# LayerNorm gains and shifts folded into the weights that follow, and the first feed-forward layer in plain fp32 on 64 rows per image

## The chip, the core and the metric

The kernel runs on one core of a Trainium2 chip. A core has a matrix engine (PE, with its weight loads shown apart as PEld), a vector engine (DVE), a scalar engine (ACT), a general engine (POOL) and a queue engine (SP) that issues DMAs. Each engine runs its own instructions in order; they meet only at semaphores. The metric is the device time of one execution in microseconds, and lower is better.

## The reference, cut to what matters

Four layers follow each other on eight images of 16 by 16 positions with 64 channels. The change lies in the third and in what the fourth reads from it:

```python
# layer 3 (its end), x after the hexagonal attention
x = _layernorm(x + attn_out, g1, beta1)
ff = jax.nn.relu(x @ w1.T + b1) @ w2.T + b2      # 64 -> 256 -> 64
x = _layernorm(x + ff, g2, beta2)
# layer 4, input x, all batch norms folded as scale and shift
h = jax.nn.relu(_bn(conv1x1(x, w1) + b1))        # 64 -> 128
h = jax.nn.relu(_bn(conv3x3(h, w2, groups=32) + b2))
h = conv1x1(h, w3) + b3                          # 128 -> 64
return jax.nn.relu(x + h)
```

`_layernorm` is (x - mean) * rsqrt(var + eps) * gain + shift over the 64 channels. The first two layers are self-attentions over the 256 positions of an image.

## The kernel before

Channels lie on partitions. Two images stand above each other, image 0 of a pair on partitions 0 to 63 and image 1 on 64 to 127, so there are four pairs of 256 columns. From the end of the third layer on, two pairs make one group `gr` of 512 columns, which fills one PSUM bank. Weights of a 64 by 64 layer are laid on the diagonal of a 128 by 128 matrix, so that one matmul serves both images.

Each engine's program is written out by hand, so the order in the code is the order on the engine. Nothing is scheduled or planned by a tool.

**Preparation.** `prepare2` on PE (L925) multiplies weights together while the hexagonal attention is being prepared: `outc` (the output projection with the centring matrix), `w2c` (the second feed-forward layer with it) and the two centred biases of `cb`. ACT copies them from PSUM at L488 to L490, in front of the copy `att_hi` (L492) that the attention waits for. Behind `prepare2`, PE runs matmuls on zeros (`keep_warm`, L834), then `batch_norm_rows` (L1085), one more `keep_warm`, and then `cast` (L1052), which spreads the attention weights over the channels for DVE's `weighted_values` (L738).

**A LayerNorm,** number n = 0 to 3: 0 and 1 are the first one of groups 0 and 1, 2 and 3 the second one. PE has already put the centred input into `D_BANK[gr]`. ACT squares it (`squares`, L501), PE averages the squares over 64 channels (`variance`, L1092), ACT takes the logarithm and the exponential of minus one half of it (`inverse_std`, L507 and L511), DVE multiplies (`layer_norm`, L771, writes `xhat`) and in a second pass applies gain and shift (L774, writes `x1` or `x2`). `x2` has the place of `yT`.

**The first feed-forward layer** works on halves in the type fp32r, whose products keep fewer bits. `halves` on DVE rounds `x1` to its upper half (L783) and stores the rest (L787), for each image in a tile `xs[:, gr, i, :]` of its own: upper half on the image's own 64 partitions, rest on the other 64. The weights are split in the same way into `w1_hi` and `w1_lo`, each holding w1 twice. So for each image and each half of the 256 hidden channels two matmuls over 128 rows give the layer: eight for a group (L1104). `centre_r`, made by four ACT copies at L478, then puts the centred `x1` into `D_BANK` (L1111, two matmuls), and the second layer adds to it (L1116, plain fp32, images 0 and 1 on output partitions 0 to 63 and 64 to 127). The ReLU with bias b1 is ACT's for image 0 (L516) and DVE's for image 1 (L793).

**The fourth layer.** `conv1` (L1128, weights `c1s` = w1 times the batch norm's scale), ReLU on ACT into `strips` with 32 partitions at a time (`conv1_out`, L529), two shifted copies for each strip on DVE (`shifts`, L307), the 3 by 3 convolution as four column tiles of 32 outputs (`conv2`, L1140, and `conv2_last`, L1150), ReLU on ACT (L541, L536), `conv3` (L1163), and `finish` on DVE, which adds bias and `x2` (L807) and takes the ReLU (L810). There are three results: columns 0 to 511, and twice 256 columns, each with its own store. The programs of PE, ACT and DVE from the first LayerNorm on end in lists of calls (L1184 to L1207, L545 to L562, L812 to L825).

Of the kernel before, what the change touches and what calls it, by code (L numbers as in the profile page):

```python
# [14 lines left out]
F32 = mybir.dt.float32  # L15
# [51 lines left out]
def build(nc, t, out):  # L67

    ctx = ExitStack()
    with ctx:  # L70
# [47 lines left out]
        centre_r = ctx.enter_context(nc.sbuf_tensor("centre_r", [128, 2, 128], F32R))  # L118
# [38 lines left out]
        w1_hi = ctx.enter_context(nc.sbuf_tensor("w1_hi", [128, DFF], F32R))  # L157
        w1_lo = ctx.enter_context(nc.sbuf_tensor("w1_lo", [128, DFF], F32R))


        xs = ctx.enter_context(nc.sbuf_tensor("xs", [128, GROUPS, 2, 512], F32R))
# [3 lines left out]
        xhat = sb("xhat", 128, 2, 512)  # L165
        x1 = sb("x1", 128, GROUPS, 512)
        x2 = yT[:, :, :].rearrange("p (g j) n -> p g (j n)", g=GROUPS)
# [13 lines left out]
        x3 = sq[:, :, :].rearrange("p a n -> p (a n)")  # L181
# [41 lines left out]
        xhat_sb, ln_out = sem("xhat_sb"), sem("ln_out")  # L223
        stacked = sem("stacked")
        w1_split, x_upper, x_lower = sem("w1_split"), sem("x_upper"), sem("x_lower")
# [72 lines left out]

        AFFINE = [("L2_conv_g1", "L2_conv_beta1"), ("L2_conv_g2", "L2_conv_beta2")]
# [82 lines left out]
        def _(act):  # L382
# [130 lines left out]
            def relu_ff(gr):  # L513
                for h in range(FH):
                    act.wait_ge(ff_ps, 2 * FH * gr + h + 1)
                    s.activation(ffh[:, gr, h, 0, :], bank[h], ACT.Relu,  # L516
                                 bias=col("L2_conv_b1", h)).then_inc(ff_act, 1)

            def conv1_out(c):

                act.wait_ge(c1_ps, c + 1)
                if c == 0:
                    act.wait_ge(bn_ready, 3)
                    act.wait_ge(zeroed, 3)
                if c >= 2:
                    act.wait_ge(c2_ps, c - 1)
                for r in range(CONV_BLOCKS):
                    h = slice(32 * r, 32 * r + 32)
                    s.activation(strips[32:64, c % 2, r, :, 1:1 + SIDE, :],  # L529
                                 bank[c][h, :].rearrange("p (j a b) -> p j a b", j=2, b=SIDE),  # L530
                                 ACT.Relu, bias=bnsh[h, 0:1]).then_inc(c1_sb, 1)
# [15 lines left out]
            squares(1)  # L547
            inverse_std(1)
            relu_ff(0)
# [15 lines left out]
        def _(dve):  # L565
# [105 lines left out]
            for n in range(SLOTS):  # L671
# [89 lines left out]
            for i in range(2):  # L761
                v.tensor_tensor(c1s[:, i, :], c1[:, i, :], bank[7][:, 0:128], ALU.mult)
# [4 lines left out]
            def layer_norm(n):  # L767
                gr = n % 2
                dst, (gain, shift) = (x1, x2)[n // 2], AFFINE[n // 2]
# [7 lines left out]
            def halves(gr):  # L777


                dve.wait_ge(ln_out, gr + 1)  # L780
                for i in range(2):
                    own = slice(64 * i, 64 * i + 64)
                    v.tensor_copy(xs[own, gr, i, :], x1[own, gr, :]).then_inc(x_upper, 1)  # L783
                for i in range(2):
                    own, other = slice(64 * i, 64 * i + 64), slice(64 - 64 * i, 128 - 64 * i)
                    dve.wait_ge(x_upper, 2 * gr + i + 1)
                    v.tensor_tensor(xs[other, gr, i, :], x1[own, gr, :], xs[own, gr, i, :].bitcast(F32),  # L787
                                    ALU.subtract).then_inc(x_lower, 1)

            def relu_ff(gr):  # L790
                for h in range(FH):
                    dve.wait_ge(ff_ps, 2 * FH * gr + FH + h + 1)
                    v.tensor_scalar(ffh[:, gr, h, 1, :], bank[FH + h], col("L2_conv_b1", h), 0.0,  # L793
                                    ALU.add, ALU.max).then_inc(ff_dve, 1)
# [21 lines left out]
            halves(1)  # L816
# [11 lines left out]
        def _(pe):  # L828
# [96 lines left out]
            def prepare2():  # L925
# [8 lines left out]
                for k, name in enumerate(("L2_conv_out_b", "L2_conv_b2")):  # L934
                    ins = mm(b[:, 256 + k:257 + k], centre, col(name), start=True, stop=True)
# [142 lines left out]
            def batch_norm_rows():  # L1078
# [3 lines left out]
                for k in range(2):  # L1082
                    b = bninv[:, k:k + 1]
                    column = bass.AP(tensor=b.tensor, offset=b.offset, ap=[list(b.ap[0]), [0, 128]])
                    ins = mm(bank[7][:, 128 * k:128 * k + 128], column, ident, start=True, stop=True)  # L1085
                ins.then_inc(bnrow_ps, 1)
# [7 lines left out]
            def feed_forward1(gr):  # L1094

                pe.wait_ge(w1_split, 2)
                pe.wait_ge(stacked, 1)
                for i in range(2):
                    pe.wait_ge(x_lower, 2 * gr + i + 1)
                    for h in range(FH):  # L1100
                        if gr:
                            pe.wait_ge(ff_act if i == 0 else ff_dve, h + 1)
                        for w in (w1_hi, w1_lo):
                            ins = mm(bank[FH * i + h], w[:, 128 * h:128 * h + 128], xs[:, gr, i, :],  # L1104
                                     start=w is w1_hi, stop=w is w1_lo)
                        ins.then_inc(ff_ps, 1)

            def feed_forward2(gr):

                for i in range(2):  # L1110
                    mm(D_BANK[gr], centre_r[:, i, :], xs[:, gr, i, :], start=i == 0, stop=False)  # L1111
# [9 lines left out]
            def conv1(c):  # L1121
                gr, i = c // 2, c % 2
                pe.wait_ge(ln_out, 3 + gr)
# [4 lines left out]
                mm(bank[c], c1s[:, i, :], x2[:, gr, :], start=True, stop=True).then_inc(c1_ps, 1)  # L1128
# [25 lines left out]
            def conv3(n, i):  # L1154

                b, columns = RESULTS[n]
                gr = n > 0
                if i == 0:
                    pe.wait_ge(c2_sb, 2 * gr + 1)
                else:  # L1160
                    pe.wait_ge(c2_sb, n + gr + 2)
                c2 = c2out.rearrange("p g i n -> p i g n")[:, i, gr, columns.start - 512 * gr:columns.stop - 512 * gr]
                ins = mm(b[64 * i:64 * i + 64, :], table["c3"], c2, start=True, stop=True)  # L1163
# [22 lines left out]
            out_sums(3)  # L1186
            variance(1)
            feed_forward1(0)
            feed_forward2(0)
            variance(2)  # L1190
            feed_forward1(1)
# [98 lines left out]
```

## Time and profile before

| | us |
|---|---|
| median of 3 runs | 128.46 |
| lowest and highest | 128.42, 128.50 |
| span of the profiled execution | 125.2 |

The profile is of one execution, and its span runs from the first to the last instruction. The time of that execution itself isn't listed; what lies around the span is taken as the median minus the span, 3.26 us. The granted clock of PE is 1.000 over the whole span.

| engine | busy us | share of the span | instructions |
|---|---|---|---|
| PE | 105.7 | 84% | 600 |
| DVE | 93.7 | 75% | 246 |
| ACT | 68.5 | 55% | 164 |
| POOL | 42.7 | 34% | 43 |

The chain that ended last (followed back from the last instruction, at each step to what released it) is PE for 42% of the span, DVE for 29% and ACT for 15%. PE's busy time counts overlapping records, so what a change is worth is read from the chain and the timeline of the stage, not from these shares. A plain fp32 matmul shows as two MATMUL records, one in fp32r as one. A time in the timeline is the start from the span's beginning, and the duration reaches to the end of the last record of a row.

### The profile page before, as it was taken

The page shows a single profiled execution, that of the slowest core. Times are in us where ns is not written, and L with a number is a line of the kernel's source. Part 1 is how long each engine was busy: PE and PEld are TensorE (multiplying, and loading weights), DVE is VectorE, ACT ScalarE, POOL GpSimd, SP SyncE. Part 2 cuts the span into 40 slices and gives each one's busy share as a digit, 9 for nine tenths or more (in the row PEclk, how much of TensorE's full clock was granted, in tenths as well). Part 3 has the DMA queues.
Part 4 walks back from the last instruction along what each step waited for, and adds up shares of the span by engine and source line. Part 5 has one row for each costly group of instructions (what it writes and reads, how often), then busy time and mean ns, then how long its engine had stood idle before and what let it go on. Part 6 is the DMA issues. An engine that isn't in the chain of part 4 may idle for free.

```text
span 125.2 us, 1845 instructions
## 1 busy us (share of the span) xinstructions
PE 105.7 (84%) x600; PEld 64.4 (51%) x600; DVE 93.7 (75%) x246; ACT 68.5 (55%) x164; POOL 42.7 (34%) x43
## 2 busy tenths in 40 slices
PE   4988999899999988599399957998697992998990
PEld 1475957577777775365035634985353530221350
DVE  1078999878888669737979989793878739998733
ACT  3137985687979775637503310025534579986530
POOL 8996004351608217095500079991000000000000
PEclk9999999999999999999999999999999999999999
DMA  3960000000000000000000000000000000000022
GB/s 105 309 280 0 0 0 0 5 5 0 0 0 0 0 5 0 0 0 0 5 0 0 0 3 0 0 0 0 0 0 0 0 5 3 0 0 0 5 84 84
DMA packets 1593, 2.81 MB, mean 22 GB/s; under 512 B 176, under 2 KB 1200, under 8 KB 1584
## 3 DMA queue, kind: packets, MB, share of 16 engines
q1 hardware_dynamic: 1152, 2.02, 4.5%
q10 hardware_dynamic: 432, 0.67, 1.6%
q8 instruction: 5, 0.08, 0.3%
q14 instruction: 4, 0.03, 0.1%
HBM read 2.17 MB, written 0.52 MB: 22 GB/s over the span
## 4 chain that ended last, share of the span: by engine, by line
PE 42%; DVE 29%; ACT 15%; issue 8%; DMA 2%; POOL 1%; ACTq 0%; DVEq 0%
PE bank L913 5%; DVE strips L307 5%; PE bank L883 4%; DVE probn L604 4%; ACT prob L411 4%; PE bank L1074 3%; PE bank L1104 3%; DVE ffh L253 3%; PE bank L1116 3%; PE bank L1052 3%; ACT strips L529 3%; DVE nmax L595 3%; DMA p<-in_p 2%; PE duo L1140 2%; DVE qkprod L738 2%
## 5 line engine op out<-in xcount | busy, mean ns | idle before, releaser
L411 ACT ACTIVATE prob<-bank,nmax 128x256 f32<-128x256 f32 x32 | 14.8, 469 | 8.2 <-DVE nmax L595 7.8
L883 PE MATMUL bank<-kz,q 128*128 128x256 f32 x64 | 16.4, 383 | 0.3 <-ACT kz L400 0.3
L595 DVE TENSOR_REDUCE nmax<-bank 128x2 f32<-128x512 f32 x16 | 11.0, 689 | 5.7 <-PE bank L883 5.7
L307 DVE COPY strips<-strips 32x480 f32<-32x480 f32 x32 | 12.8, 400 | 3.0 <-ACT strips L529 2.4
L883 PEld LDWEIGHTS bank<-kz,q 128*128 128x128 f32 x64 | 11.5, 190 | 2.1 <-issue 0.5
L604 DVE TENSOR_SCALAR probn<-prob,rrec 128x256 f32<-128x256 f32 x32 | 12.1, 421 | 0.6
L529 ACT ACTIVATE strips<-bank,bnsh 32x512 f32<-32x512 f32 x16 | 10.9, 680 | 2.1 <-PE duo L1140 1.1
L893 PE MATMUL bank<-pv,probn 128*128 128x128 f32 x64 | 10.0, 278 | 2.1 <-DVE probn L604 2.1
L501 ACT ACTIVATE sq<-bank,cb 128x512 f32<-128x512 f32 x4 | 2.7, 687 | 15.3 <-PE bank L1074 11.0
L1140 PE MATMUL duo<-strips,ctaps 128*32 128x512 f32 x72 | 8.3, 596 | 3.2 <-DVE strips L307 3.2
L893 PEld LDWEIGHTS bank<-pv,probn 128*128 128x128 f32 x64 | 7.4, 142 | 4.6 <-DVE probn L604 4.2
L418 ACT ACTIVATE probT<-bank 128x512 f32<-128x512 f32 x16 | 9.4, 596 | 0.1
L346 POOL TENSOR_TENSOR grs<-gvar,minus_half 128x1 f32<-128x1 f32 x4 | 2.7, 683 | 19.2 <-DVE gvar L626 19.2
L913 PE MATMUL bank<-probT,v 128*64 128x256 f32 x64 | 8.5, 390 | 1.0 <-ACT probT L418 1.0
L253 POOL TENSOR_TENSOR qkprod<-q,k 128x768 f32<-128x768 f32 (+1 forms) x4 | 5.8, 1469 | 9.0 <-ACT k L443 9.0
L1052 PE MATMUL bank<-att_hi,head_cast_r 128*128 128x448 f32 x16 | 6.7, 420 | 2.4 <-POOL att_lo L260 1.5
L1140 PEld LDWEIGHTS duo<-strips,ctaps 128*32 128x32 f32 x72 | 2.0, 109 | 9.3 <-DVE strips L307 5.8
L834 PE MATMUL bank<-zeros 128*128 128x512 f32 x8 | 5.1, 741 | 1.6 <-DVE zeros L575 1.6
L411 ACT ACTIVATION_READ_ACCUMULATOR prob<-bank,nmax 128x1 f32 x32 | 6.3, 197 | 0.0
L738 DVE TENSOR_TENSOR ffh<-bank,v 128x128 f32<-128x128 f32 (+1 forms) x24 | 5.5, 304 | 0.6 <-PE bank L1052 0.6
L913 PEld LDWEIGHTS bank<-probT,v 128*64 128x64 f32 x64 | 4.0, 136 | 3.7 <-ACT probT L418 2.1
L1052 PE MATMUL bank<-att_lo,head_cast_r 128*128 128x448 f32 x16 | 5.8, 365 | 0.0
(148 smaller groups left out, 229.3 us busy)
## 6 DMA issues: line engine op xcount, KB each, us to landing
p<-in_p SPq DMA_DIRECT2D x1, 952.0 KB, 7.1
xT<-in_xT SPq DMA_DIRECT2D x4, 128.0 KB, 4.0
p<-in_p ACTq DMA_DIRECT2D x1, 448.0 KB, 5.7
out_dram<-xT SPq DMA_DIRECT2D x1, 256.0 KB, 2.0
out_dram<-xT SPq DMA_DIRECT2D x2, 128.0 KB, 1.7
pv<-in_pv ACTq DMA_DIRECT2D x1, 128.0 KB, 3.2
p<-in_p ACTq DMA_DIRECT2D x1, 79.5 KB, 3.0
```

Of the source, the lines that this page charges most:

```text
L253: return engine.tensor_tensor(products[j][:, k0:k0 + n, :].rearrange("p k (a b) -> p k a b", b=SIDE), rep(q2[:, j, :].rearrange("p (a b) - ...
L307: return engine.tensor_copy(strips[32 * s:32 * s + 32, c % 2, r, :, 1:1 + SIDE, d], strips[32:64, c % 2, r, :, 1:1 + SIDE, f])
L411: s.activation(prob[:, n % 3, b, :], S_BANK[n % 3][:, b * TOK:(b + 1) * TOK], ACT.Exp, bias=nmax[:, n, b:b + 1], accum_out=rsum[:, n, b:b ...
L418: s.activation(flat(probT[:, n % 4, :, :]), T_BANK[n % 2], ACT.Copy).then_inc(probT_sb, 1)
L529: s.activation(strips[32:64, c % 2, r, :, 1:1 + SIDE, :], bank[c][h, :].rearrange("p (j a b) -> p j a b", j=2, b=SIDE), ACT.Relu, bias=bns ...
L595: v.tensor_reduce(nmax[:, n, :], S_BANK[n % 3].rearrange("p (b m) -> p b m", b=BLK), AX.X, ALU.max, negate=True).then_inc(max_ready, 1)
L604: v.tensor_scalar(probn[:, n % 2, b, :], prob[:, n % 3, b, :], rrec[:, n, b:b + 1], None, ALU.mult).then_inc(norm_done, 1)
L883: ins = mm(S_BANK[n % 3][:, b * TOK:(b + 1) * TOK], q[:, b * 128:b * 128 + 128], k, start=True, stop=True)
L893: ins = nc.tensor.transpose(T_BANK[n % 2][:, mb * TOK + b * 128:mb * TOK + b * 128 + 128], probn[:, n % 2, b, mb * 128:mb * 128 + 128], ident)
L913: ins = mm(OUT_BANK[p][64 * i:64 * i + 64, 0:TOK], val[:, 2 * j + mb, 64 * i:64 * i + 64], probT[:, (2 * p + i) % 4, mb, :], start=mb == 0 ...
L1052: ins = mm(CAST_BANKS[m % 2][h][:, 0:NB * 64], w, flat(a[:, c, :, :]), start=a is att_hi, stop=a is att_lo)
L1140: ins = mm(bank[7 - c % 2][32 * r:32 * r + 32, :], ctaps[:, r, ty, :], strips[:, c % 2, r, :, ty:ty + SIDE, :], start=ty == 0, stop=ty == 2)
```

## The change

The gain and the shift of both LayerNorms leave the data and go into weights and biases:

- `w1g` = w1 times gain 1, and `b1f` = b1 plus w1 times shift 1. `centre_g` = the centring matrix times gain 1, and shift 1 is added to the centred bias in `cb`. `c1s` also gets gain 2, and `bnsh1` is the batch norm's shift with shift 2 worked in. `gain2` is a diagonal matrix with gain 2, and `b3f` is the last bias plus shift 2.
- The second DVE pass of each LayerNorm (L774) is gone, and `xhat` keeps all four results.
- `halves`, `w1_hi`, `w1_lo`, `xs` and `centre_r` are gone. The first feed-forward layer is four plain fp32 matmuls for a group, each over the 64 rows of one image, with images 0 and 1 on different rows and in different banks. One fp32 matmul with `centre_g` replaces the two at L1111.
- `conv3` starts each result with a matmul of `gain2` and `xhat`, so `finish` is one DVE instruction instead of two.
- `prepare2` gets three more small matmuls, `batch_norm_rows` one, and ACT two copies into `b1f`.
- On PE, `feed_forward1(0)` goes ahead of `variance(1)` and `feed_forward1(1)` ahead of `variance(2)`. On ACT, `relu_ff(0)` goes ahead of `inverse_std(1)`.

The diff, cut to its core:

```diff
@@ ACT
-            act.wait_ge(tables_in["p1"], 16)
-            for i in range(2):
-                for half in range(2):
-                    h = slice(64 * half, 64 * half + 64)
-                    ins = s.activation(centre_r[h, i, :], centre[64 * i:64 * i + 64, :], ACT.Copy)
-            ins.then_inc(stacked, 1)
...
                     s.activation(cb[:, 0:2], PREP_BANK[:, 256:258], ACT.Copy).then_inc(prep2_sb, 1)
+                    for h in range(FH):
+                        s.activation(b1f[:, h:h + 1], PREP_BANK[:, 258 + h:259 + h], ACT.Identity,
+                                     bias=col("L2_conv_b1", h)).then_inc(affine_b, 1)
...
             squares(1)
+            relu_ff(0)
             inverse_std(1)
-            relu_ff(0)
             squares(2)
@@ DVE
-                    v.tensor_copy(w1_hi[:, :], table["w1T"]).then_inc(w1_split, 1)
-                    dve.wait_ge(w1_split, 1)
-                    v.tensor_tensor(w1_lo[:, :], table["w1T"], w1_hi[:, :].bitcast(F32), ALU.subtract)\
-                        .then_inc(w1_split, 1)
+                    v.tensor_scalar(w1g[:, :], table["w1T"], col("L2_conv_g1"), None, ALU.mult)
+                    v.tensor_scalar(centre_g[:, :], centre, col("L2_conv_g1"), None, ALU.mult)
+                    v.tensor_scalar(gain2[:, :], ident, col("L2_conv_g2"), None, ALU.mult)
+                    v.tensor_tensor(b3f[:, :], col("L3_conv_b3"), col("L2_conv_beta2"), ALU.add)\
+                        .then_inc(affine_w, 1)
...
-                v.scalar_tensor_tensor(out=xhat[:, gr, :], in0=D_BANK[gr], scalar=cb[:, n // 2:n // 2 + 1],
+                v.scalar_tensor_tensor(out=xhat[:, n, :], in0=D_BANK[gr], scalar=cb[:, n // 2:n // 2 + 1],
                                        in1=rstd[:, gr, :], op0=ALU.add, op1=ALU.mult).then_inc(xhat_sb, 1)
-                dve.wait_ge(xhat_sb, n + 1)
-                v.tensor_scalar(dst[:, gr, :], xhat[:, gr, :], col(gain), col(shift), ALU.mult, ALU.add)\
-                    .then_inc(ln_out, 1)
...
-                done(v.scalar_tensor_tensor(out=x3[:, columns], in0=b, scalar=col("L3_conv_b3"),
-                                            in1=x2.rearrange("p g n -> p (g n)")[:, columns],
-                                            op0=ALU.add, op1=ALU.add))
-                v.tensor_scalar(fin[:, columns], x3[:, columns], 0.0, None, ALU.max).then_inc(fin_sb, 1)
+                v.tensor_scalar(fin[:, columns], b, b3f[:, :], 0.0, ALU.add, ALU.max).then_inc(fin_sb, 1)
 
             layer_norm(0)
-            halves(0)
             relu_ff(0)
@@ PE
-                for k, name in enumerate(("L2_conv_out_b", "L2_conv_b2")):
-                    ins = mm(b[:, 256 + k:257 + k], centre, col(name), start=True, stop=True)
+                mm(b[:, 256:257], centre, col("L2_conv_out_b"), start=True, stop=True)
+                mm(b[:, 257:258], centre, col("L2_conv_b2"), start=True, stop=False)
+                mm(b[:, 257:258], centre, col("L2_conv_beta1"), start=False, stop=True)
+                for h in range(FH):
+                    ins = mm(b[:, 258 + h:259 + h], table["w1T"][0:64, 128 * h:128 * h + 128],
+                             col("L2_conv_beta1")[0:64], start=True, stop=True)
...
+                mm(bank[7][:, 256:257], c1[0:64, 0, :], col("L2_conv_beta2")[0:64], start=True, stop=True)\
+                    .then_inc(bnrow_ps, 1)
...
-                for i in range(2):
-                    pe.wait_ge(x_lower, 2 * gr + i + 1)
-                    for h in range(FH):
-                        if gr:
-                            pe.wait_ge(ff_act if i == 0 else ff_dve, h + 1)
-                        for w in (w1_hi, w1_lo):
-                            ins = mm(bank[FH * i + h], w[:, 128 * h:128 * h + 128], xs[:, gr, i, :],
-                                     start=w is w1_hi, stop=w is w1_lo)
-                        ins.then_inc(ff_ps, 1)
+                for h in range(FH):
+                    if gr:
+                        pe.wait_ge(ff_act, h + 1)
+                        pe.wait_ge(ff_dve, h + 1)
+                    for i in range(2):
+                        own = slice(64 * i, 64 * i + 64)
+                        ins = mm(bank[FH * i + h], w1g[own, 128 * h:128 * h + 128], xhat[own, gr, :],
+                                 start=True, stop=True)
+                    ins.then_inc(ff_ps, 1)
...
-                for i in range(2):
-                    mm(D_BANK[gr], centre_r[:, i, :], xs[:, gr, i, :], start=i == 0, stop=False)
+                mm(D_BANK[gr], centre_g[:, :], xhat[:, gr, :], start=True, stop=False)
...
+                own = slice(columns.start - 512 * gr, columns.stop - 512 * gr)
                 if i == 0:
+                    mm(b, gain2[:, :], xhat[:, 2 + gr, own], start=True, stop=False)
                     pe.wait_ge(c2_sb, 2 * gr + 1)
```

The order on PE, from the last matmuls of the attention into the feed-forward stage of group 0, before:

```order
L1074 MATMUL bank<-prob,outc 128x256 x2
L1092 MATMUL duo<-sq,p 128x512 [waits lnv_sb,sq_sb]
L1104 MATMUL bank<-xs,w_hi 128x512 [waits x_lower,stacked,w1_split]
L1104 MATMUL bank<-xs,w_lo 128x512
L1104 MATMUL bank<-xs,w_hi 128x512
L1104 MATMUL bank<-xs,w_lo 128x512
L1104 MATMUL bank<-xs,w_hi 128x512 [waits x_lower]
L1104 MATMUL bank<-xs,w_lo 128x512
L1104 MATMUL bank<-xs,w_hi 128x512
L1104 MATMUL bank<-xs,w_lo 128x512
L1111 MATMUL bank<-xs,centre_r 128x512 x2
L1116 MATMUL bank<-ffh,w2c 64x512 [waits ff_dve,ff_act]
```

The same place after, through to the variance of LayerNorm 2 (`duo<-sq,p` is a variance, `w1g` the first layer, `w2c` the second):

```order
L1053 MATMUL bank<-prob,outc 128x256 x2
L1084 MATMUL bank<-xhat,w1g 128x512 [waits xhat_sb,affine_w]
L1084 MATMUL bank<-xhat,w1g 128x512 x3
L1072 MATMUL duo<-sq,p 128x512 [waits lnv_sb,sq_sb]
L1090 MATMUL bank<-xhat,centre_g 128x512
L1095 MATMUL bank<-ffh,w2c 64x512 [waits ff_dve,ff_act]
L1095 MATMUL bank<-ffh,w2c 64x512
L1095 MATMUL bank<-ffh,w2c 64x512 [waits ff_dve,ff_act]
L1095 MATMUL bank<-ffh,w2c 64x512
L1084 MATMUL bank<-xhat,w1g 128x512 [waits ff_act,ff_dve,xhat_sb,affine_w]
L1084 MATMUL bank<-xhat,w1g 128x512
L1084 MATMUL bank<-xhat,w1g 128x512 [waits ff_dve,ff_act]
```

The variance of LayerNorm 1 has moved from ahead of the first layer to behind it, and the variance of LayerNorm 2 stands two rows behind the last one printed here, behind the first layer of group 1.

The order on ACT from the squares of LayerNorm 2 on is the same in both; after, it reads:

```order
L490 ACTIVATE sq<-bank,cb 128x512 [waits var_ps,d_ps]
L496 ACTIVATE lnv<-duo,epsln 128x512 [waits var_ps]
L500 ACTIVATE rstd<-lnv 128x512 [waits xhat_sb,lnv_sb]
L507 ACTIVATE ffh<-bank,b1f 128x512 [waits ff_ps] x2
L490 ACTIVATE sq<-bank,cb 128x512 [waits var_ps,d_ps]
```

The two ReLUs of group 1 (the row with `ffh`) stand behind the logarithm and the exponential of LayerNorm 2, which wait for that variance.

The end of PE's program after (`gain` is `gain2`; before, the three rows with it are not there, and the rest is the same):

```order
L1119 MATMUL duo<-strips,ctaps 32x512 x11
L1139 MATMUL bank<-xhat,gain 128x512
L1144 MATMUL bank<-ffh,p 64x512 [waits c2_sb] x2
L1129 MATMUL bank<-strips,ctaps 32x256 [waits shifted]
L1129 MATMUL bank<-strips,ctaps 32x256 x23
L1139 MATMUL bank<-xhat,gain 128x256
L1144 MATMUL bank<-ffh,p 64x256 [waits c2_sb] x2
L1139 MATMUL bank<-xhat,gain 128x256
L1144 MATMUL bank<-ffh,p 64x256 [waits c2_sb] x2
```

Each matmul with the gain stands directly ahead of the `conv3` of its result, behind all convolutions that precede it.

## Rows read from the trace of the kernel before

**Rows 1.** Chain that ended last, in order of time: start us, length us, what.
```profile
86.82 0.76 DVE xhat L771
...
87.61 0.56 DVE x L774
...
88.19 0.42 DVE xs L783
...
89.10 0.70 DVE xs L787
...
89.93 2.09 PE bank L1104 x8
...
94.46 0.70 ACT sq L501
...
95.20 1.12 PE duo L1092 x2
96.33 1.88 PE bank L1104 x8
...
98.68 1.94 PE bank L1116 x8
```

**Rows 2.** Timeline of PE: start, us, engine, line, operation [idle before <-releaser].
```profile
84.38 1.02 PE L1092 MATMUL duo<-sq,p 128*128 128x512 f32 x2
...
105.82 2.78 PE L1140 MATMUL duo<-strips,ctaps 128*32 128x512 f32 x24 [2.43 <-DVE strips L307]
108.53 1.98 PE L1128 MATMUL bank<-yT,c1s 128*128 128x512 f32 x4
```

**Rows 3.** Records of one line each, L1140 and L1092: duration ns min/median/max.
```profile
L1140 PE MATMUL duo<-strips,ctaps x72: 592/592/617, 105.8 to 116.2; 128*32 128x512 f32 x72
...
L1092 PE MATMUL duo<-sq,p x8: 592/592/697, 84.4 to 101.9; 128*128 128x512 f32 x8
```

**Rows 4.** Timeline of ACT, group 1 of the feed-forward layer.
```profile
96.36 0.69 ACT L507 ACTIVATE lnv<-duo,epsln 128x512 f32<-128x512 f32 x1 [1.22 <-PE duo L1092]
...
97.62 1.25 ACT L516 ACTIVATE ffh<-bank,p 128x512 f32<-128x512 f32 x2
```

**Rows 5.** Timeline of all engines, the preparation and the start of the attention.
```profile
66.81 0.56 PE L935 MATMUL bank<-p 128*128 128x1 f32 x4
...
67.22 1.96 PE L834 MATMUL bank<-zeros 128*128 128x512 f32 x4
...
68.71 0.58 ACT L492 ACTIVATE att_hi<-att 128x448 fp32r<-128x448 f32 x1 [0.80 <-DVE att L725]
...
69.35 0.68 PE L1085 MATMUL duo<-pv,bninv 128*128 128x128 f32 x4 [0.17 <-DVE sexp L716]
```

**Rows 6.** Timeline of DVE alone, the weighted values of the attention.
```profile
71.94 2.73 DVE L738 TENSOR_TENSOR qkprod<-bank,v 128x192 f32<-128x192 f32 x12
75.07 2.73 DVE L738 TENSOR_TENSOR qkprod<-bank,v 128x192 f32<-128x192 f32 x12 [0.41 <-PE bank L1052]
```

**Rows 7.** Timeline of all engines, the convolutions of the fourth layer.
```profile
107.28 6.72 DVE L307 COPY strips<-strips 32x480 f32<-32x480 f32 x16
...
109.70 2.80 ACT L529 ACTIVATE strips<-bank,bnsh 32x512 f32<-32x512 f32 x4 [0.29 <-PE bank L1128]
...
114.05 2.78 PE L1140 MATMUL duo<-strips,ctaps 128*32 128x512 f32 x24 [0.59 <-DVE strips L307]
```

**Rows 8.** Timeline of all engines, the end.
```profile
116.77 1.45 PE L1163 MATMUL bank<-ffh,p 128*64 128x512 f32 x4
...
118.15 2.80 PE L1150 MATMUL bank<-strips,ctaps 128*32 128x256 f32 x48
...
120.88 1.31 PE L1163 MATMUL bank<-ffh,p 128*64 128x256 f32 x8
...
122.31 0.48 DVE L807 SCALAR_TENSOR_TENSOR sq<-bank,p,yT 128x256 f32<-128x256 f32 x1
122.82 0.29 DVE L810 TENSOR_SCALAR xT<-sq 128x256 f32<-128x256 f32 x1
```

More of the change, by code:

```diff
@@ L116, in build @@
         c1s = sb("c1s", 128, 2, CM)
-        centre_r = ctx.enter_context(nc.sbuf_tensor("centre_r", [128, 2, 128], F32R))
+        centre_g = sb("centre_g", 128, 128)
+        gain2 = sb("gain2", 128, 128)
+        b1f = sb("b1f", 128, FH)
+        b3f = sb("b3f", 128, 1)
+        bnsh1 = sb("bnsh1", 128, 1)
         ctaps = sb("ctaps", 128, CONV_BLOCKS, 3, 32)
@@ L164, in build @@
         rstd = sb("rstd", 128, 2, 512)
-        xhat = sb("xhat", 128, 2, 512)
-        x1 = sb("x1", 128, GROUPS, 512)
-        x2 = yT[:, :, :].rearrange("p (g j) n -> p g (j n)", g=GROUPS)
+        xhat = sb("xhat", 128, 2 * GROUPS, 512)
         ffh = sb("ffh", 128, 2, FH, 2, 512)
@@ L530, in conv1_out @@
                                  bank[c][h, :].rearrange("p (j a b) -> p j a b", j=2, b=SIDE),
-                                 ACT.Relu, bias=bnsh[h, 0:1]).then_inc(c1_sb, 1)
+                                 ACT.Relu, bias=bnsh1[h, :]).then_inc(c1_sb, 1)
             def conv2_out_last():
@@ L761, in _ @@
             for i in range(2):
-                v.tensor_tensor(c1s[:, i, :], c1[:, i, :], bank[7][:, 0:128], ALU.mult)
+                v.scalar_tensor_tensor(out=c1s[:, i, :], in0=c1[:, i, :], scalar=col("L2_conv_g2"),
+                                       in1=bank[7][:, 0:128], op0=ALU.mult, op1=ALU.mult)
+            v.scalar_tensor_tensor(out=bnsh1[:, :], in0=bank[7][:, 256:257], scalar=bninv[:, 0:1],
+                                   in1=bnsh[:, 0:1], op0=ALU.mult, op1=ALU.add)
             v.tensor_tensor(ctaps[:, :, :, :], ctap,
@@ L768, in layer_norm @@
                 gr = n % 2
-                dst, (gain, shift) = (x1, x2)[n // 2], AFFINE[n // 2]
                 dve.wait_ge(rstd_sb, n + 1)
-                v.scalar_tensor_tensor(out=xhat[:, gr, :], in0=D_BANK[gr], scalar=cb[:, n // 2:n // 2 + 1],
+                v.scalar_tensor_tensor(out=xhat[:, n, :], in0=D_BANK[gr], scalar=cb[:, n // 2:n // 2 + 1],
                                        in1=rstd[:, gr, :], op0=ALU.add, op1=ALU.mult).then_inc(xhat_sb, 1)
-                dve.wait_ge(xhat_sb, n + 1)
-                v.tensor_scalar(dst[:, gr, :], xhat[:, gr, :], col(gain), col(shift), ALU.mult, ALU.add)\
-                    .then_inc(ln_out, 1)
-            def halves(gr):
-                dve.wait_ge(ln_out, gr + 1)
-                for i in range(2):
-                    own = slice(64 * i, 64 * i + 64)
-                    v.tensor_copy(xs[own, gr, i, :], x1[own, gr, :]).then_inc(x_upper, 1)
-                for i in range(2):
[L785 to L788, printed above, removed]
             def relu_ff(gr):
+                if gr == 0:
+                    dve.wait_ge(affine_b, FH)
                 for h in range(FH):
-                    dve.wait_ge(ff_ps, 2 * FH * gr + FH + h + 1)
-                    v.tensor_scalar(ffh[:, gr, h, 1, :], bank[FH + h], col("L2_conv_b1", h), 0.0,
+                    dve.wait_ge(ff_ps, FH * gr + h + 1)
+                    v.tensor_scalar(ffh[:, gr, h, 1, :], bank[FH + h], b1f[:, h:h + 1], 0.0,
                                     ALU.add, ALU.max).then_inc(ff_dve, 1)
@@ L1084, in batch_norm_rows @@
                     column = bass.AP(tensor=b.tensor, offset=b.offset, ap=[list(b.ap[0]), [0, 128]])
-                    ins = mm(bank[7][:, 128 * k:128 * k + 128], column, ident, start=True, stop=True)
-                ins.then_inc(bnrow_ps, 1)
+                    mm(bank[7][:, 128 * k:128 * k + 128], column, ident, start=True, stop=True)
+                mm(bank[7][:, 256:257], c1[0:64, 0, :], col("L2_conv_beta2")[0:64], start=True, stop=True)\
+                    .then_inc(bnrow_ps, 1)
             def variance(n):
@@ L1094, in feed_forward1 @@
             def feed_forward1(gr):
[L1096 to L1106 removed]
+                pe.wait_ge(affine_w, 1)
+                pe.wait_ge(xhat_sb, gr + 1)
+                for h in range(FH):
[7 more added lines that the diff above has]
+                    ins.then_inc(ff_ps, 1)
             def feed_forward2(gr):
[L1110 to L1111 removed]
+                mm(D_BANK[gr], centre_g[:, :], xhat[:, gr, :], start=True, stop=False)
                 for h in range(FH):
@@ L1127, in conv1 @@
                     pe.wait_ge(ff_dve, 4)
-                mm(bank[c], c1s[:, i, :], x2[:, gr, :], start=True, stop=True).then_inc(c1_ps, 1)
+                mm(bank[c], c1s[:, i, :], xhat[:, 2 + gr, :], start=True, stop=True).then_inc(c1_ps, 1)
             def conv2(c):
@@ L1161, in conv3 @@
                     pe.wait_ge(c2_sb, n + gr + 2)
-                c2 = c2out.rearrange("p g i n -> p i g n")[:, i, gr, columns.start - 512 * gr:columns.stop - 512 * gr]
-                ins = mm(b[64 * i:64 * i + 64, :], table["c3"], c2, start=True, stop=True)
+                c2 = c2out.rearrange("p g i n -> p i g n")[:, i, gr, own]
+                ins = mm(b[64 * i:64 * i + 64, :], table["c3"], c2, start=False, stop=True)
                 if i:
```

26 lines of the change are left out of this document (11 added, 15 removed).

## The prediction, made before the changed kernel ran

> **What bounds the kernel now.** I read the page's chain first, then the chain in order of time through the last third, then the timelines around each edit. The engines take turns, so an edit pays only where it is the link that ends last. In the first feed-forward stage that link is visible work of the kind that the change removes: `xhat` of group 0 is done at 87.58, DVE then scales it, rounds it twice and subtracts twice, and the first matmul of L1104 starts at 89.93 [rows 1]. From there PE, one ACT square and PE again hold the chain to 100.62 [rows 1]. In the fourth layer DVE's copies and ACT's strips run side by side: the copies of strip set 1 end at half of the row of 6.72 us that began at 107.28, at 110.64, while ACT's first strip of set 2 is ready at about 109.70 + 0.70 = 110.40 [rows 7]. So either engine alone can give back only 0.24 there. At the end PE holds the chain from 114.05 to `conv3` of the last results, and DVE ends it at 123.11 [rows 7, 8].
>
> **Prices on PE.** A plain fp32 matmul of 512 columns is two passes. Two records in 1.02 us with 0.59 for a record [rows 2, 3] put the second start 0.43 after the first, so a matmul holds PE for 0.86, and its result is out 0.16 after that. A first pass after a pause, or after a change of the form of the tile, takes 0.10 more (0.697 against 0.592, [rows 3]). A change of form adds a gap as well: 24 records of 32 output columns start at 105.82 and hold six slots of 0.43, to 108.40, and the next form starts at 108.53 [rows 2]. Together a change costs about 0.2. Column tiles of one form overlap fully: those 24 records, four tiles wide, take 2.78 = 6 x 0.43 + the rest [rows 2], and the eight of L1116 take 1.94 [rows 1].
>
> **The first feed-forward layer.** Before, it is eight passes of about 0.23 for a group, 1.88 in all [rows 1]. After, it is four fp32 matmuls over 64 rows, eight passes of 0.43. No row of this trace has a matmul over 64 rows. If the two images, on different rows and in different banks, overlap as the column tiles do, that is four slots, 1.72. If not, it is 3.44. A gain beyond that would need a pass over 64 rows to be shorter than one over 128. I take the overlap, because the nearest rows, L1116 and L1140, overlap two and four deep. The page TensorE: Matmul & The Clock Gate of the Trainium skill (Part 3) says that row tiles overlap too, with 3.07 times measured for four. No row here shows it. At that efficiency of 0.77 a group would cost 0.5 more, an estimate, and the sum would be 130.8.
>
> **Group 0 and group 1 in a row.** DVE's 0.56, 0.42 and 0.43, 0.70 and the rest go: the first matmul moves from 89.93 to about 87.66 [rows 1], 2.27 earlier. What comes behind it on PE is new:
> - first layer, 0.10 + 1.72, to 89.48
> - variance 1, which stood ahead of it: 0.2 + 0.86, to 90.54 (its ACT and DVE steps are off the chain: about 2.4 us to `xhat` 1 at 92.9, needed at 93.4)
> - `centre_g` in fp32: 0.86 instead of two fp32r passes, to 91.40
> - second layer: 0.2 + 1.72, to 93.32, out at 93.48, so ACT's square starts 0.96 earlier than 94.46 [rows 1]
> - first layer of group 1: 0.2 + 1.72, to 95.24
> - variance 2, which now waits for it: 0.2 + 0.86 + 0.16, out at 96.46, against 95.20 + 1.12 = 96.32 before [rows 1].
>
> So by variance 2 the 2.27 are gone and it is 0.14 later. ACT has the logarithm, the exponential and only then the two ReLUs that the second layer waits for, starting 1.26 after the logarithm [rows 4]. The first ReLU ends at about 98.43, PE starts the second layer at 98.5 instead of 98.68 and ends it at 100.4 instead of 100.62. **Net gain 0.2.** What is late next is ACT.
>
> **Fourth layer.** The second DVE pass at 106.70 goes, 0.55, but ACT's first strip ends the wait after 0.24. I take a further gain of 0.2, so the last full convolution starts about 0.4 earlier than 114.05 [rows 7].
>
> **The gain matmuls at the end.** Before, the last convolution pair starts 118.15 - 114.05 = 4.10 after that point [rows 7, 8]. After, PE has six slots (2.58), a change (0.2), `gain2` (0.86), a change (0.2), `conv3` with both images overlapping (0.86; before, image 1 waited for ACT) and 0.1: 4.80. **Loss 0.7.** Nothing hides it: the matmul stands behind the convolution though its inputs are ready long before. Passes of 256 columns hold 0.22 (24 slots' worth of two: 48 records, four wide, in 2.80 [rows 8]). From 120.88, the start of the last `conv3` group, to the end at 122.82 + 0.29 = 123.11 it was 2.23 [rows 8]. After: a gain matmul (0.48), change and `conv3` (0.1 + 0.48), gain matmul (0.58), `conv3` (0.58), 0.2 until DVE starts, and one DVE instruction from PSUM. For that I take 0.48, the row of the PSUM read; the other bound is 0.29, the row from SBUF [rows 8]. That makes 2.9. **Loss 0.67,** or 0.48 at the lower bound. `finish` loses an instruction for each result, but PE, not DVE, is then last.
>
> **The preparation.** DVE's four instructions for weights replace two, at a place where it waits for PE; ACT's four `centre_r` copies go where it is idle. Both are nothing. `prepare2` gets six passes more. Four records hold 67.22 - 66.81 = 0.41 [rows 5], so 0.6, and two changes of form 0.3: the zero matmuls then end at 69.9 and not ahead of the wait that ends at 69.35 [rows 5]. `batch_norm_rows` adds a 64-row matmul, 0.2 and two changes 0.3. The first `cast` comes 1.0 later. It had about 0.2 of slack before DVE's weighted values at 71.94, and DVE waits 0.41 more before 75.07 [rows 6], which absorbs half of what is left. **Loss 0.4,** with bounds 0 and 1.0. ACT's two copies of one column in front of `att_hi` at 68.71 [rows 5] eat its 0.80 of idle time and about 0.2 more, on the same stretch, so they don't add.
>
> **The sum.** Against the profiled execution: -0.2 - 0.2 + 0.7 + 0.67 + 0.4 = +1.4, a span of 126.6. With the 3.26 around it, which no edit touches, that is 129.8, set against the median of 128.46. With changes of form for nothing it would be about 129.0, with twice their price 131.0. The page TensorEngine Tiling of the Trainium skill (Key Properties) says that a change of tiling mode drains the engine. The gap in the rows agrees for column forms; for row forms nothing shows it.
>
> **Rivals.**
> - *Images don't overlap.* Each group's first layer takes 3.44, and both are on the chain: +3.4, 133.2. For it: no row shows 64-row tiles. Against: both column forms overlap. Chance 0.12.
> - *Faster: passes over 64 rows are cheap.* The one mechanism that can turn the sign is the pass price of L1104's successor. If a 64-row pass held 0.21 instead of 0.43, both groups would be 0.86 shorter, and variance 2 would come 1.7 earlier. Then 129.8 - 1.7 = 128.1. It decides from a pass of 0.25 down. Against: matmuls with 32 and with 128 weight columns have the same record, 0.592 [rows 3], so the 512 streamed columns set it and not the share of the array in use. Chance 0.08.
> - *No change: the preparation hides and changes cost nothing.* -0.4 and -0.8: 128.6. Chance 0.08.
> - *The change doesn't do what it says.* DVE does lose its instructions, so only the compiler could merge the images on the same rows. That is the first rival.
>
> **How the numbers follow.** The forecast, 129.8, has 0.72, with its own range of 128.9 to 131.0. The range from 128.1 to 131.0 takes in the faster and the unchanged case, and leaves out the 0.12 without overlap and some of the forecast's edges. About 0.2% (0.26 us) is what a measurement can tell from no change. Faster by more than that: 0.10. Within it: 0.10. Slower: 0.80.
>
> **What would show it.** Right: the first-layer matmuls start near 87.7 plus the delay of the preparation, in pairs; variance 2 comes out behind group 1's first layer, no earlier than before; about 0.7 more between the last full convolution and the last pair; DVE's last instruction waits for PE. Wrong: single 64-row matmuls one after the other (133), or pairs in slots shorter than 0.43 (128), or the first `cast` no later than before.

## The result, and the profile after

The changed kernel is slower: a median of 130.26 us over 13 executions (128.53 to 131.90), against 128.59 us (128.31 to 130.78) for 13 of the kernel before. Taken over the executions of each kernel that are at most 1.5% above its fastest, the ratio is 1.0108 with a 95% interval of 1.0065 to 1.0151.

In most executions of either kernel PE's clock is granted at its lower level (1.2 instead of 2.4 GHz) for one or more stretches, each costing 0.7 to 1.8 us, so spans are compared below for executions with PE at full clock, beside the medians. At full clock the kernel before has a span of 125.2 (the profile shown ahead of the prediction, and two executions measured later, of 126.96 and 127.01 us), the changed one 126.7. The change costs 1.5 us.

The changed kernel's profile has a granted clock of 0.996 and a time of 128.53 us, so 1.8 us lie around its span. The changed kernel's busy times:

```profile
PE 109.7 (87%) x614; PEld 64.5 (51%) x614; DVE 87.0 (69%) x234; ACT 67.6 (53%) x162; POOL 42.8 (34%) x43
```

DVE is 6.7 us less busy and PE 4.0 more. In the chain that ended last, PE went from 42% to 54% of the span. The chain in order of time through the feed-forward stage, which answers [rows 1] (start, length, what):

```profile
87.25 0.76 DVE xhat L765
...
88.15 1.99 PE bank L1084 x8
90.14 1.06 PE duo L1072 x2
91.20 0.86 PE bank L1090 x2
92.05 1.87 PE bank L1095 x8
93.92 1.92 PE bank L1084 x8
95.84 1.07 PE duo L1072 x2
...
96.93 0.70 ACT lnv L496
...
98.91 1.94 PE bank L1095 x8
100.85 1.07 PE bank L1107 x2
```

L1084 is the first layer, L1072 a variance, L1090 the centring and L1095 the second layer. `xhat` of group 0 ends at 88.0, 0.43 later than before, and the first layer starts 0.14 behind it, where it took 2.35 before. From there PE works without a gap to 96.9. Then it waits for ACT, whose logarithm and exponential stand ahead of the ReLUs, and `conv1` follows at 100.85, where it followed at 100.62 before. `xhat` was 0.43 later and `conv1` is 0.23 later, so of the 2.2 us that the first layer gained only 0.2 are left.

The records of the first layer, over 64 rows:

```profile
L1084 PE MATMUL bank<-xhat,w1g x16: 589/589/693, 88.2 to 95.2; 64*128 64x512 f32 x16
```

A pass over 64 rows is as long as one over 128 (0.592 in [rows 3]), and eight of them take 1.99 where eight of them one after the other, 0.43 apart, would take 3.6. So the images overlap in pairs.

The end, which answers [rows 7] and [rows 8] (timeline, the rows of PE, and the last one of DVE):

```profile
114.11 2.78 PE L1119 MATMUL duo<-strips,ctaps 128*32 128x512 f32 x24 [0.65 <-DVE strips L301]
116.82 1.13 PE L1139 MATMUL bank<-xhat,gain 128*128 128x512 f32 x2
117.88 1.08 PE L1144 MATMUL bank<-ffh,p 128*64 128x512 f32 x4
118.89 2.80 PE L1129 MATMUL bank<-strips,ctaps 128*32 128x256 f32 x48
121.61 0.70 PE L1139 MATMUL bank<-xhat,gain 128*128 128x256 f32 x2
122.24 0.65 PE L1144 MATMUL bank<-ffh,p 128*64 128x256 f32 x4
122.83 0.70 PE L1139 MATMUL bank<-xhat,gain 128*128 128x256 f32 x2
123.45 0.65 PE L1144 MATMUL bank<-ffh,p 128*64 128x256 f32 x4
...
124.16 0.48 DVE L787 TENSOR_SCALAR xT<-bank,b3f 128x256 f32<-128x256 f32 x1 [0.73 <-PE bank L1144]
```

From the last full convolution to the pair behind it, L1129, it is 4.78 instead of 4.10. From the start of L1129 to the end it is 5.75 instead of 4.96. Those two are all of the 1.5, since the last full convolution itself starts only 0.06 later than before: the 0.43 lost by `xhat` has been regained on the way, 0.2 in the feed-forward stage and 0.2 in the fourth layer.

### The profile page after: what moved, and what is told of

Same layout as the page of the kernel before. It is cut to its first block, busy times and chain, and to the rows that moved or that the text cites. A ratio compares the mean times of both kernels' runs of the same rounds, so it can differ in the third digit from the quotient of the medians.

```text
span 126.7 us, 1861 instructions
## 1 busy us (share of the span) xinstructions
PE 109.7 (87%) x614; PEld 64.5 (51%) x614; DVE 87.0 (69%) x234; ACT 67.6 (53%) x162; POOL 42.8 (34%) x43
## 4 chain that ended last, share of the span: by engine, by line
PE 54%; DVE 24%; ACT 12%; issue 7%; ACTq 0%; DVEq 0%
DVE strips L301 5%; PE bank L888 5%; PE duo L1119 4%; PE bank L858 4%; DVE qkprod L730 4%; PE bank L809 4%; DVE probn L595 4%; ACT prob L405 3%; PE bank L1053 3%; DVE ffh L249 3%; PE bank L1084 3%; PE bank L1095 3%; PE bank L1031 3%; DVE nmax L586 3%; PE duo L1072 2%
## 5 line engine op out<-in xcount | busy, mean ns | idle before, releaser
L765 DVE SCALAR_TENSOR_TENSOR xhat<-bank,cb,rstd 128x512 f32<-128x512 f32 x4 | 3.0, 750 | 5.6 <-ACT rstd L500 5.4
```

## The experiments

A span "at full clock" is that of the executions whose mean granted clock is at least 0.995. Medians depend on how many executions had stretches at the lower clock, so they say less than these spans; they are given too.

### The end alone: finish_on_dve

```diff
@@ PE, conv3
-                    mm(b, gain2[:, :], xhat[:, 2 + gr, own], start=True, stop=False)
@@ DVE, finish
-                v.tensor_scalar(fin[:, columns], b, b3f[:, :], 0.0, ALU.add, ALU.max).then_inc(fin_sb, 1)
+                done(v.scalar_tensor_tensor(out=x3[:, columns], in0=xhat[:, 2 + gr, own], scalar=col("L2_conv_g2"),
+                                            in1=b, op0=ALU.mult, op1=ALU.add))
+                v.tensor_scalar(fin[:, columns], x3[:, columns], b3f[:, :], 0.0, ALU.add, ALU.max).then_inc(fin_sb, 1)
```

> The changed kernel without its three gain matmuls; gain 2 is applied by DVE in the last step instead (two DVE instructions per result, as in the kernel before). If the gain matmuls are 0.7 us ahead of the last convolution pair and cost the same again behind it, the span falls from 126.7 by 0.7 + 0.78 = 1.5 to about 125.2, and the last instruction of DVE waits for DVE again. Rival: DVE's second instruction per result was what the end waited for, and only the 0.7 comes back (126.0).

Span at full clock 125.3 (one execution of 12, 127.07 us), 1.4 less than the changed kernel. The median is 130.31 (ratio to the kernel before 0.998, interval 0.9934 to 1.0027), because 7 of the 12 had a mean clock of 0.971 to 0.973 and spans of 128.4 to 128.7. The profile is of an execution with a stretch at the lower clock ahead of this place, so its times are later, but the distances hold. Timeline:

```profile
115.77 2.78 PE L1124 MATMUL duo<-strips,ctaps 128*32 128x512 f32 x24 [0.65 <-DVE strips L302]
...
119.81 2.80 PE L1134 MATMUL bank<-strips,ctaps 128*32 128x256 f32 x48
...
124.54 0.35 DVE L792 TENSOR_SCALAR xT<-sq,b3f 128x256 f32<-128x256 f32 x1
```

From the full convolution to the pair it is 4.04 (4.78 in the changed kernel), and from there to the end 5.08 (5.75). Both terms of the gain matmuls come back, 0.74 and 0.67, with DVE carrying two instructions per result again. The rival, that only 0.7 returns, falls.

### ACT's order alone: relu_first

```diff
@@ ACT
             squares(2)
+            relu_ff(1)
             inverse_std(2)
-            relu_ff(1)
```

> The changed kernel with one line moved on ACT: the two ReLUs of group 1 stand ahead of the logarithm and exponential of LayerNorm 2. In the changed kernel's trace the first layer of group 1 is out at 94.98 and 95.84 and ACT is idle from 94.66 to 96.93, while PE waits 1.16 us, to 98.91, for the ReLU. If ACT's order eats the earlier start, the second layer starts at about 97.7 and the span falls by 1.2 to 125.5. Rival: PE's order (the variance behind the first layer) is the bound; then LayerNorm 2 still ends at 99.06 and the gain is below 0.3.

Span at full clock 125.5, 125.5 and 125.7 in three executions of 12, so 1.0 to 1.2 less; median 128.97 (ratio to the kernel before 0.9964, interval 0.9911 to 1.0016). One line takes back what the earlier start had lost. Its place is read best in the profile of both_undone_filled below, which has the same edit and full clock. Timeline of ACT, then of PE:

```profile
94.99 0.69 ACT L508 ACTIVATE ffh<-bank,b1f 128x512 f32<-128x512 f32 x1 [0.37 <-PE bank L1090]
95.85 0.69 ACT L508 ACTIVATE ffh<-bank,b1f 128x512 f32<-128x512 f32 x1 [0.17 <-PE bank L1090]
96.89 0.69 ACT L497 ACTIVATE lnv<-duo,epsln 128x512 f32<-128x512 f32 x1 [0.36 <-PE duo L1078]
```

```profile
95.73 1.12 PE L1078 MATMUL duo<-sq,p 128*128 128x512 f32 x2
96.69 1.02 PE L1096 MATMUL bank<-xhat,centre_g 128*128 128x512 f32 x2
97.64 1.94 PE L1101 MATMUL bank<-ffh,w2c 128*64 128x512 f32 x8
```

Both ReLUs fit into ACT's idle time before the logarithm, which starts when it did in the changed kernel, and the second layer starts at 97.64 instead of 98.91. The rival falls: PE's own order, with the variance behind the first layer, was not what ended last.

### The overlap of the 64-row matmuls: rows128

The weights of each image are padded with zeros to 128 rows, so each matmul takes the rows of both images and multiplies those of the other one by zero.

```diff
+                        v.tensor_scalar(w1g[own, i, :], table["w1T"][own, :], col("L2_conv_g1")[own], None, ALU.mult)
...
-                        ins = mm(bank[FH * i + h], w1g[own, 128 * h:128 * h + 128], xhat[own, gr, :],
+                        ins = mm(bank[FH * i + h], w1g[:, i, 128 * h:128 * h + 128], xhat[:, gr, :],
```

> The changed kernel with the first feed-forward layer over all 128 rows: the weights of each image are padded with zeros on the other image's rows, so no two of its matmuls can overlap; everything else stays. If the 64-row pairs overlap fully, each group needs 3.44 us instead of 1.72, less about 0.4 for the changes of form that fall away: the span grows by 3.0 to 3.4, to about 129.9. Rival: the 64-row matmuls overlap only in their records and the difference is below 1.5.

Span at full clock 129.7 in one execution of 6, 3.0 more (131.47 us; median 134.11, ratio to the kernel before 1.0314, interval 1.0235 to 1.0393). The profile is of another execution, whose granted clock is 1.00 from 86 to 106 us. The chain's two pieces:

```profile
89.78 3.67 PE bank L1087 x8
...
97.03 3.63 PE bank L1087 x8
```

They are 1.68 and 1.71 longer than in the changed kernel. The variances behind them are 0.2 shorter each, as no change of form lies between. The rival of less than 1.5 falls. So rows of one image each, in separate banks, overlap fully in plain fp32.

### The preparation alone: prepare_only

This is the kernel before, with the small matmuls and ACT's two copies added and their results unused.

```diff
+                mm(b[:, 260:261], centre, col("L2_conv_beta1"), start=True, stop=True)
+                for h in range(FH):
+                    ins = mm(b[:, 258 + h:259 + h], table["w1T"][0:64, 128 * h:128 * h + 128],
+                             col("L2_conv_beta1")[0:64], start=True, stop=True)
...
+                mm(bank[7][:, 256:257], c1[0:64, 0, :], col("L2_conv_beta2")[0:64], start=True, stop=True)\
...
+                    for h in range(FH):
+                        s.activation(b1f[:, h:h + 1], PREP_BANK[:, 258 + h:259 + h], ACT.Identity,
+                                     bias=col("L2_conv_b1", h))
```

> The kernel before with only the preparation of the change added (three small matmuls in prepare2, one in batch_norm_rows, two one-column copies on ACT; their results are not used). If the preparation alone costs what the changed kernel's trace shows at the first variance of LayerNorm, the span grows by 0.3 to 0.45 from that of the kernel before. Rival: it is covered by DVE's 0.41 us of waiting and costs under 0.1.

Span at full clock 125.6 in one execution, 0.4 more. In the nine with a clock of 0.985 to 0.987 it is 127.0 to 127.4, median 127.1, against 125.9 to 126.8, median 126.7, in 15 of the kernel before. The rival, less than 0.1, falls. The median of all is no help here (128.89 against 128.90, ratio 1.0012, interval 0.9977 to 1.0048), since the number of stretches at the lower clock moves it more than 0.4.

### Both mended, and the waits of PE filled: both_undone, both_undone_filled, before_filled, after_filled

both_undone is the changed kernel with the edits of finish_on_dve and relu_first. The three others are both_undone, the kernel before and the changed kernel, each with matmuls on zeros put where PE waits:

```diff
+            keep_warm(bank[5], 2)
             head_sums(1)
...
             conv1(1)
+            keep_warm(bank[7], 2)
             conv2(0)
```

> The changed kernel with both mends together: gain 2 applied by DVE in the last step, and group 1's ReLUs ahead of LayerNorm 2's logarithm on ACT. Alone they took the span at full clock from 126.7 to 125.3 and 125.5. If they are separate terms of one chain they add: 124.1 at full clock, 1.1 below the 125.2 of the kernel before. Rival: the 1.2 of the ReLUs is given back by ACT or DVE in the convolutions once the end is short, and the span stays above 124.8.

> As both_undone, with matmuls on zeros put into PE's two long waits: two ahead of the second head_sums (PE idles 2.06 us there in the kernel before) and two ahead of the first 3 by 3 convolution (2.43 us). They take 1.8 us each time and delay nothing. In the profiles in which a stretch was granted half the clock, it began at 62.7 to 63.6 or at 106.4 to 111.4, right behind one of these waits. If the waits cause it, most executions keep the full clock, the span stays at 124.1 and the median falls to about 126. Rival: the chip grants the half clock for another reason (the load), the executions spread as before, and the median is 127.5 or more.

> The kernel before with the same four matmuls on zeros in the same two waits. If the waits cause the half clock, the median falls from 128.5 or 128.9 to 127.0 to 127.3 (the full-clock span of 125.2 plus the 1.8 around it); if not, it stays within 0.3 of 128.6.

> The changed kernel with the same four matmuls on zeros. If the waits cause the half clock, the median falls from 130.3 to about 128.6 (span 126.7), and the difference to before_filled is the change's cost at equal clock, 1.5. If not, it stays near 130.2.

| kernel | span at full clock | median us | executions at full clock |
|---|---|---|---|
| both_undone | 124.1 | 127.57 | 2 of 6 |
| both_undone_filled | 124.1 | 125.88 | 6 of 6 |
| before_filled | 125.2 | 127.01 | 10 of 12 |
| after_filled | 126.7 | 128.51 | 12 of 12 |
| the kernel before, same chip | 125.2 | 128.55 | 1 of 23 |

The two mends add to 2.6, with nothing given back, so with both the change is 1.1 faster than the kernel before at full clock. The filled waits leave the span at full clock as it is, and make full clock the rule, so the rival, another reason for the lower clock, falls. The rows by stretch show it (columns: stretch, its length, busy us of PE, PEld, DVE, ACT and POOL with their instructions, then the granted clock, the DMA share and GB/s), first of finish_on_dve, whose waits are open:

```profile
102.00:106.00 4.00, 1.59 (x4) 0.38 (x2) 3.20 (x8) 3.87 (x6) 0.00 (x0) 1.00 0.01 2
106.00:110.00 4.00, 3.98 (x24) 1.03 (x24) 3.71 (x9) 2.79 (x5) 0.00 (x0) 0.57 0.00 0
```

and of after_filled:

```profile
102.00:106.00 4.00, 3.31 (x8) 1.14 (x6) 3.20 (x8) 3.87 (x6) 0.00 (x0) 1.00 0.00 2
106.00:110.00 4.00, 3.97 (x27) 1.35 (x28) 3.70 (x9) 3.59 (x7) 0.00 (x0) 1.00 0.00 0
```

With PE busy for 1.59 of 4 us the next stretch is granted 0.57 on average; with 3.31 it is granted all. The wait makes the lower clock likely and not certain, for the profile of the kernel before has the same open wait and keeps the full clock:

```profile
102.00:106.00 4.00, 1.57 (x8) 0.48 (x10) 3.29 (x9) 3.84 (x7) 0.00 (x0) 1.00 0.01 2
106.00:110.00 4.00, 4.00 (x28) 1.20 (x20) 3.80 (x9) 3.61 (x6) 0.00 (x0) 1.00 0.00 0
```

The profile of before_filled is one of its two with such a stretch, and shows a third place, behind PE's wait for DVE's halves:

```profile
86.00:90.00 4.00, 2.33 (x9) 1.05 (x7) 2.99 (x6) 2.34 (x5) 0.00 (x0) 1.00 0.00 0
90.00:94.00 4.00, 4.00 (x12) 2.73 (x12) 1.94 (x4) 1.82 (x3) 0.00 (x0) 0.57 0.00 0
```

There PE waits 0.78 ahead of the variance and 0.90 behind it in the kernel before; in the changed one it waits 0.59 in all, and all 12 executions of after_filled keep the full clock. after_filled against before_filled, 128.51 to 127.01, is the cleanest measure of the change: 1.5 us. The third place is shown by one profile only, so its share in before_filled is argued, not shown.

### One matmul on zeros less: filled_one_warm

This is both_undone_filled with one matmul on zeros less behind `prepare2`.

```diff
-        WARM_UP, WARM_SOFTMAX, WARM_SOFTMAX2 = 1, 2, 1
+        WARM_UP, WARM_SOFTMAX, WARM_SOFTMAX2 = 1, 1, 1
```

> As both_undone_filled, with one matmul on zeros instead of two behind prepare2 on PE. In both_undone_filled the first cast starts at 71.30, and DVE's weighted values wait for it until 72.7. If the preparation's cost lies in PE being late at the first cast, it starts 0.86 earlier and DVE at about 72.1, where the attention weights bind: the second cast pair still needs POOL's att_lo, so the span falls by 0.15 only, to 124.0, and the rest of the preparation's 0.4 is ACT's two copies ahead of att_hi. Rival: PE's lateness is all of it, and the span falls by 0.4 to 123.7.

The span is 123.8 in five of six executions (124.2 in one), 0.3 less, and the first row below starts 0.26 earlier. That lies between the two numbers, and both stories missed the link. Rows of POOL, of both_undone_filled and then of this kernel:

```profile
74.20 1.02 POOL L369 TENSOR_TENSOR avsum<-qkprod 128x384 f32<-128x384 f32 x1 [0.19 <-DVE qkprod L731]
```

```profile
73.94 1.01 POOL L369 TENSOR_TENSOR avsum<-qkprod 128x384 f32<-128x384 f32 x1
```

In the kernel before this row starts at 73.80. From it on POOL adds without a pause. PE's last matmuls for group 0, behind which the first variance stands, wait for POOL's sixth unit of sums. Rows of POOL and PE, of the kernel before:

```profile
82.47 0.46 POOL L378 TENSOR_TENSOR prob<-prob,ffh 128x128 f32<-128x128 f32 x1
82.98 1.16 PEld L1074 LDWEIGHTS bank<-prob,outc 128*128 128x128 f32 x6 [0.24 <-POOL prob L378]
82.98 1.56 PE L1074 MATMUL bank<-prob,outc 128*128 128x256 f32 x6
```

and of the changed one:

```profile
82.90 0.46 POOL L372 TENSOR_TENSOR prob<-prob,ffh 128x128 f32<-128x128 f32 x1
83.42 1.56 PE L1053 MATMUL bank<-prob,outc 128*128 128x256 f32 x6
```

PE starts 0.05 and 0.06 behind POOL's end. So the first weighted values of DVE, late because of the first cast, moved POOL by 0.40 (0.42 in the changed kernel), and POOL moved the variance. With one matmul less 0.14 remains: the first `att_hi` on ACT starts at 68.83 instead of 68.71, the second at 72.19 instead of 72.05, and POOL's `att_lo` behind it is 0.14 later. This is the best version: a median of 125.65 us against 128.44 of the kernel before on the same chip, ratio 0.9815, interval 0.9774 to 0.9857. At full clock it is 1.4 faster (123.8 against 125.2); the rest comes from the clock.

### One wait filled: before_one_wait_filled

This is the kernel before with the first of the two edits above, `keep_warm(bank[5], 2)` ahead of `head_sums(1)`, alone.

> The kernel before with only the first of its two waits filled (two matmuls on zeros ahead of the second head_sums). If each wait has its own chance of a stretch at half clock, executions with two or three such stretches become rare and those with one (span 126.5 to 126.7) or none (125.2) remain, with a median of 127.0 to 128.5. If one filled wait is enough, the spans are as in before_filled (10 of 12 at 125.2). If it does nothing, spans above 127.4 stay as frequent as in the kernel before (15 of 30).

Spans 125.2, 126.6, 126.7, 126.7, 126.9 and 128.1: one at full clock, four with one stretch (clock 0.986 to 0.987), one with two (0.972), median 128.49. In the kernel before beside it, 5 of 11 were at 127.5 or above and the median was 128.44. So one filled wait is not enough, and the median did not move. That it removes part of the stretches fits the one in six at 127.5 or above, but six executions don't show it.

## Why the prediction was right

The time was forecast at 129.8 with a range of 128.1 to 131.0, and is 130.26. At full clock the forecast span of 126.6 stands against 126.7, and four of the five terms of the sum came out for the reason given. The preparation's came out by another path, and the time around the span was right by luck.

**The first layer.** The overlap was taken from column tiles; the 64-row records confirm it, with 1.99 for a group against 1.72 + 0.10 + 0.16. The rival without overlap, forecast at 3.4 more, is what rows128 ran: 3.0 more, since the variance behind each group's first layer gets 0.2 shorter there. The rival with cheap passes fell with the record of 0.589. What the Trainium skill's page TensorE: Matmul & The Clock Gate (Part 3) gives for four row tiles, 3.07 times, would have made it slower by 0.5 a group, an estimate. The two tiles in fp32 here overlap without that loss (1.99 a group).

**The row of steps.** Measured from the first matmul of the first layer, variance 1 was to start 2.0 later, and the second layer 3.9; the timeline has 1.9 and 3.8. ACT was named as what is late next, with a net gain of 0.2; the trace has PE waiting 1.16 for it, and relu_first gave 1.0 to 1.2 of it back in the span. The text did not see that ACT was idle from 94.66 to 96.93 in that plan, so that an edit of one line would keep about 1.2.

**The fourth layer.** Forecast 0.2. DVE's copies of set 1 end at 110.27 and wait 0.43 for ACT:

```profile
110.71 3.35 DVE L301 COPY strips<-strips 32x480 f32<-32x480 f32 x8 [0.43 <-ACT strips L520]
```

Before, ACT was 0.24 ahead of DVE at this place [rows 7]; now DVE is ahead of ACT, and the step gains its 0.2.

**The end.** Forecast 0.7 and 0.67; measured 0.68 and 0.79. The second was sized 0.12 too small: with 256 columns it is 0.63 and 0.62 from the start of `gain2` to that of the next `conv3`, not 0.58, and 0.71 from the last `conv3` to DVE, not 0.68. The 0.48 taken for DVE's one instruction was right.

**The preparation.** Forecast 0.4, measured 0.43 at the first variance and 0.4 by prepare_only. The size was right and the mechanism only in part, so here the number was lucky. The first cast is 1.0 later as forecast (71.31 against 70.33), DVE's weighted values start at 72.73 instead of 71.94, and DVE's wait of 0.41 is gone: PE's next cast behind them starts at 78.16 instead of 77.86, only 0.3 later. But that was not what ended last. POOL's sums, which start on DVE's first result and never pause, carried 0.42 to the end of the attention. The text named DVE and ACT and never followed POOL.

**The time around the span.** This step was wrong, and luck hid it. The 3.26 us were a median with a stretch at the lower clock minus a span without one; what lies around a span is 1.8. The forecast difference was right, and the median of the changed kernel contains the same kind of stretch, so the error cancelled. The three executions of the changed kernel at full clock took 128.53 to 128.63, 1.2 below the forecast.

**Changes of form.** For the row form the trace now shows their price: 1.92 for L1084 at 93.92, right behind the second layer, and 1.06 for the variance behind it instead of 0.87, so 0.2 each time, as for column forms. The page TensorEngine Tiling of the Trainium skill (Key Properties), which the prediction cited, says that a change of tiling mode drains the engine; the trace agrees for the row form with these 0.2.

## What to carry to other kernels

When a step gets faster in one engine's program, look where that engine's and its neighbours' hand-written order now makes them wait: here one line on ACT held 1.2 us of a 2.2 us gain. A matmul that folds an affine step into an accumulation is work for its engine: behind the last convolutions, where PE ends last, it cost 1.4 us here. Whether it costs nothing in a place where PE waits was not tried. And compare profiles at equal granted clock: the stretches that follow the two PE waits of 2.1 and 2.4 us cost 0.7 to 1.8 us each, and four matmuls on zeros in the waits took 1.5 us off the median and added nothing to the span.

## What was not expected of the hardware

The lower clock comes when PE is working again and not during the wait. In finish_on_dve PE's wait ends at 106.02 and the lower clock starts between 106.0 and 106.5; in relu_first the wait ends at 106.43 and the lower clock starts at about 107.5. In the kernel before, 22 of the 23 executions beside the filled kernels had at least one stretch at 1.2 GHz, at mean clocks of 0.959 to 0.987 and spans of 125.9 to 128.9; with two waits filled 10 of 12 had none. The cost is not the same for each: spans of 125.9 and 126.6 both occur at 0.985. That this depends on whether PE is what ends last there is likely but not shown. Only a fully granted profile can be laid beside another line by line.
